# Second product of an attention kernel: low parts once for four units, not once for two

## The reference

```python
qkv = conv1d_same(group_norm(xf, gn_gamma, gn_beta), qkv_w, qkv_b)   # 3*256 x 256 x 16 taps
q, k, v = jnp.split(qkv, 3, axis=1)
w = jnp.einsum('bct,bcs->bts', q * scale, k * scale)                 # scores, 1024 x 1024 a head
w = jax.nn.softmax(w, axis=-1)
h = jnp.einsum('bts,bcs->bct', w, v)                                 # the second product
h = conv1d_same(h, proj_w, proj_b)
```

## Time and profile before

| | before |
|---|---|
| median of 3 runs | 1106.17 us (1106.09 to 1107.38) |
| profiled execution | 1104.99 us, of which span 1103.2 us |
| PE busy | 987.4 us, 90% |
| DVE busy | 716.3 us, 65% |
| ACT busy | 650.2 us, 59% |
| POOL busy | 233.4 us, 21% |
| mean granted TensorE clock | 0.965 |

### The profile page before, as it was taken

How to read it: one execution, slowest core, us unless ns; L and a number is a source line. 1 busy time by engine, 2 the same in 40 slices (tenths; PEclk the granted TensorE clock), 3 DMA queues, 4 the chain that set the end, 5 groups by cost and what they waited for, 6 DMA issues and landing times.

```text
span 1103.2 us, 18112 instructions
## 1 busy us (share of the span) xinstructions
PE 987.4 (90%) x7250; PEld 684.0 (62%) x7250; DVE 716.3 (65%) x1222; ACT 650.2 (59%) x1049; POOL 233.4 (21%) x164
## 2 busy tenths in 40 slices
PE   2888649999999999999598999999999999988864
PEld 1555526667766776667366666766677668766654
DVE  5988557654775577668466555465536665777767
ACT  4673617664676477767565565465636575665532
POOL 2736122100330132124050000010001004313320
PEclk9998879999999999999799999999999999999987
DMA  7050033593459357737644284537445873453522
GB/s 272 13 180 1 1 125 65 99 212 68 91 111 247 51 118 168 165 67 146 171 77 86 47 185 106 87 63 182 93 67 110 201 167 73 97 124 59 115 58 77
DMA packets 284515, 122.59 MB, mean 111 GB/s; under 512 B 268304, under 2 KB 270736, under 8 KB 283536
## 3 DMA queue, kind: packets, MB, share of 16 engines
q1 hardware_dynamic: 284432, 121.44, 49.5%
HBM read 34.24 MB, written 15.87 MB: 45 GB/s over the span
## 4 chain that ended last, share of the span: by engine, by line
PE 59%; DVE 11%; ACT 8%; issue 7%; DMA 2%; POOL 1%; SPq 0%; ACTq 0%; POOLq 0%; DVEq 0%
PE cM L1049 15%; PE cQ L1049 14%; PE cP L1049 13%; PE psT L1118 4%; PE psV L1095 4%; PE psS L1118 4%; PE psV L1099 3%; ACT arena L909 2%; DVE smx L1495 2%; DVE W L1280 1%; DMA arena<-arena 1%; DVE arena L1472 1%; PE cM L990 1%; ACT arena L921 1%; PE cP L990 1%
## 5 line engine op out<-in xcount | busy, mean ns | idle before, releaser
L1049 PE MATMUL cP<-U,W 128*128 128x256 f16 (+1 forms) x1536 | 224.3, 303 | 13.8 <-DVE W L1280 12.5
L1049 PE MATMUL cM<-U,W 128*128 128x256 f16 (+1 forms) x1536 | 223.3, 301 | 11.4 <-DVE U L1309 7.4
L1049 PE MATMUL cQ<-U,W 128*128 128x256 f16 (+1 forms) x1536 | 225.6, 302 | 5.7 <-DVE W L1280 3.5
L1049 PEld LDWEIGHTS cP<-U,W 128*128 128x128 f16 x1536 | 150.7, 98 | 82.0 <-issue 11.6
L1049 PEld LDWEIGHTS cM<-U,W 128*128 128x128 f16 x1536 | 149.6, 98 | 81.1 <-issue 8.9
L1049 PEld LDWEIGHTS cQ<-U,W 128*128 128x128 f16 x1536 | 149.7, 98 | 74.2 <-issue 6.0
L1472 DVE SCALAR_TENSOR_TENSOR arena<-arena,smx 128x1024 f16<-128x1024 f32 x128 | 178.5, 1394 | 1.3 <-ACT arena L921 0.6
L902 ACT ACTIVATE smx<-smx,esc 128x1 f32<-128x1 f32 x128 | 37.5, 293 | 207.4 <-DVE smx L1495 207.0
L921 ACT ACTIVATE arena<-arena,smx 128x1024 f16<-128x1024 f32 x128 | 147.0, 1148 | 4.2
L1495 DVE TENSOR_REDUCE smx<-psS 128x1 f32<-128x1024 f32 x64 | 77.9, 1217 | 71.5 <-PE psS L1118 71.1
L1495 DVE TENSOR_REDUCE smx<-psT 128x1 f32<-128x1024 f32 x64 | 78.0, 1219 | 57.1 <-PE psT L1118 56.7
(11 more groups left out here) (212 smaller groups left out, 1202.1 us busy)
## 6 DMA issues: line engine op xcount, KB each, us to landing
staging<-w_qkv SPq DMA_DIRECT2D x20, 512.0 KB, 5.1
kept_u<-U SPq DMA_DIRECT2D x4, 2077.0 KB, 10.0
U<-kept_u SPq DMA_DIRECT2D x16, 519.2 KB, 4.4
arena<-x_tok SPq DMA_DIRECT2D x8, 512.0 KB, 6.4
arena<-arena SPq DMA_DIRECT2D x16, 256.0 KB, 3.8
W<-x_tok SPq DMA_DIRECT2D x4, 1024.0 KB, 6.1
out_tok<-W SPq DMA_DIRECT2D x3, 1024.0 KB, 4.3
kept_h<-arena SPq DMA_DIRECT2D x4, 514.0 KB, 4.2
```

The costliest lines, as they stand in the source:

```text
L1049: last = mm(out, W[:, j, wl, c, wat + tap, :], U[:, slot, ul, c, at:at + width], start=(c == 0 and tap == 0 and wl + ul == 0), stop=(c == ...
```

## The change

An even h does its 8 full-width matmuls and returns. The odd h does its own 8, and then the 64-column ones of both halves, 16 in a row. No matmul is added or left out. The start flag is now set only with the first half, since a start marks all of the bank that the two halves share, and the first half's sum is still open when the second begins. `pv_done` is counted by 2 at the odd h in place of 1 at each. Nothing else is changed: the waits on `pv_done` keep their values.

```diff
                 for s in range(8):
-                    mm(psV[:, at:at + QUART], vT[:, s, hd, :], probT[:, s, at:at + QUART], start=(s == 0), stop=False,
+                    mm(psV[:, at:at + QUART], vT[:, s, hd, :], probT[:, s, at:at + QUART], start=(s == 0 and at == 0), stop=False,
                        skip_group_check=True)
-                for s in range(8):
-                    R = D * (s % 2)
-                    last = mm(psV[R:R + D, at:at + QUART], vT[:, s, hd, D * hd:D * (hd + 1)], probT[:, 8 + s, at:at + QUART],
-                              start=False, stop=(s >= 6), skip_group_check=True)
-                last.then_inc(S["pv_done"], 1)
+                if h % 2 == 0:
+                    return
+                for at in (0, QUART):
+                    for s in range(8):
+                        R = D * (s % 2)
+                        last = mm(psV[R:R + D, at:at + QUART], vT[:, s, hd, D * hd:D * (hd + 1)], probT[:, 8 + s, at:at + QUART],
+                                  start=False, stop=(at > 0 and s >= 6), skip_group_check=True)
+                last.then_inc(S["pv_done"], 2)
```

## The result

| | before | after |
|---|---|---|
| median | 1106.7 us (1106.09 to 1107.38, 4 runs) | 1125.74 us (1124.51 to 1126.43, 4 runs) |
| ratio | | 1.0177, 95% interval 1.0165 to 1.019 |
| span of the profiled execution | 1103.2 us | 1122.7 us |
| PE busy | 987.4 us | 985.6 us |
| mean granted clock | 0.965 | 0.960 |

The forecast was 1117.4 us, with a range up to 1122.5. The sign and the places of the main losses were right, the size was not: +19.5 us of span in place of +11.2.

A forecast was written before the change was run, and what follows sets the result against it. PE was taken to bound runs 0, 1, 2, 4, 5 and 6. Terms -5.0 + 7.2 + 7.8 + 1.2 = +11.2 us on the profiled 1104.99, plus 1.2 for the median, gave 1117.4 us; range 1109 to 1122.5.

The forecast's parts named there:

- The saving on PE: PE, 24 groups of four units in runs 0, 1, 2, 4, 5, 6: 0.21 us saved a group, 5.0 us in all.
- The turns wait for the odd h: SP: turns 4, 8 and 12 wait two slots longer, for h = 1, 3 and 5; turn 4 starts 8 us late.
- Unit 8's wait: PE, unit 8's scores: wait 1.2 us for the copy behind late turn 4, in six runs, 7.2 us.
- Run 2: Second half of load_w(4) behind late turn 12: squares and PE's spread 5.8 us later, plus 2 for clock, 7.8 us.
- Run 3: load_w(5) behind turn 5, which waits for its own low part; PE waits there anyway: 0 (to +1) us.
- Runs 0, 1 and 6: Late turns 8 and 12 were taken as covered, their next reader four slots on; no loss counted for this.
- Run 7: Last h = 7 at half clock with four more pairs, 0.9 us, plus 0.3 for a longer h = 5: 1.2 us.
- the 0.3 for h = 5: Run 7: h = 5 gets 0.44 us longer ahead of the last unit's scores; 0.3 of it counted.
- more comes late: Bunched transfers slow one another, turn 5 misses h = 2, or clock falls: 1 us more in six runs, 1123.4; chance 0.10.

The follow-up runs named there:

- the merged order alone: Changed kernel's matmul order, but even halves' 64-column matmuls read a stable tile, with pv_done counted by 1 at each h as before: 1101.77 us, ratio 0.9967.
- the kernels with the moves: Copy, run 3's and run 2's loads, stores and reload of runs 0 and 1, run 6's residual reordered: on the changed kernel 1097.05 us, on the kernel before 1098.87.
- the three kernels with a single move: Changed kernel with one reordering: copy ahead of turn 4, 1116.14 us; run 2's load ahead of turn 12, 1120.17; run 6's residual behind turn 14, 1122.74.
- The merged kernel with the moves: Changed kernel with copy, run 3's and run 2's loads, stores and reload of runs 0 and 1, run 6's residual reordered: 1097.05 us; 1096.68 on another chip.

## Why the prediction was too low

- **The saving on PE: right.** 0.21 us a group were forecast, 0.23 measured without the waits, 0.92 us a run where PE is the bound, 0.5 us more in six runs than I had counted. The Trainium skill ("TensorEngine Tiling (Array Packing)", Key Properties) says that a change of tiling mode drains the engine; with a full drain a group would have saved 0.32 us. The measured 0.23 is below it, as the rows had said; the 0.27 us of the last matmul, on which the 0.32 rests, is an end that the profile models.
- **The turns wait for the odd h: right**, to 0.1 us.
- **Unit 8's wait: right, a little low.** 1.2 us forecast, 1.09 to 1.26 printed in runs 0, 1, 2, 4, 5, 6. But I had worked out a delay of the scores' start, and that is 1.38 us: in run 5 they start 6.08 us behind the end of h = 1 in place of 4.70. The view counts idle time from the end of the last matmul, 0.16 us (0.27 - 0.109) after the next could have started. Taking the wait away gave 1.4 us a run in runs 4 and 5. Six times the 0.2 is 1.1 us of the missing sum.
- **Run 2: right.** 5.8 us on ACT forecast, 5.56 of wait there; the whole term 7.8 forecast, 8.15 measured by taking it away. The parts were both a little low: PE's wait grew by 6.5 and not 5.8 us (0.5 of it comes with the merged order alone), and PE then worked for 4.8 us at a granted clock of 0.50 (482.2 to 487.0), which is 2.4 us lost and not 2.
- **Run 3: wrong.** The step was "The one in run 3 follows turn 5, which waits for its own low part; PE waits there anyway, and I take 0 (to +1)". Both halves failed. Turn 5 does not start much later, but it stands close behind turn 4, the copy and an input quarter, and takes 3.94 us in place of the 1.84 that it had. And the wait on PE was the effect of that very load, not a cover: ACT waited 8.0 us for it before and 10.44 after. Measured: +2.5 us.
- **Runs 0, 1 and 6: wrong, of the same kind.** The step was "Turns 8 and 12 have their next reader four slots on, as turn 4 has". I followed the late turn and not the one behind it. Once turn 12 is late, turn 13 follows it and a 1 MB load without a pause, and h = 6 waits for 13, not 12: 2.18 us in run 6. The late turn 12 alone was not enough: with the 1 MB moved away h = 6 does not wait. In runs 0 and 1 turns 10 and 11 come behind turns 8 and 9 and a 2 MB store; h = 5 waits 0.74 and 0.26 us. That these are the queue and not PE is shown by the kernels with the moves, in which all three waits are gone (and another, before h = 7 of run 6, has come with the residual). The 0.74 of run 0 stands in one trace of a run that varies by 1.1 us, but it comes again as 0.70, 0.49 and 0.48 in the three kernels with a single move.
- **Run 7: near, and in part by luck.** 1.2 us forecast, 1.8 measured, but from other parts. The last block:

```profile
1073.14 1.86 PE L1095 MATMUL psV<-arena 128*128 128x256 f16 x8 [6.49 <-DMA arena<-arena]
1074.93 1.92 PE L1102 MATMUL psV<-arena 128*64 128x256 f16 x16
```

  1.92 us for the 16 against 1.06 for the 8 in the earlier trace rows, 0.86 of the 0.9 that I counted. Of the 0.3 for h = 5 only 0.1 came: the last h = 7 starts 129.29 us after the run's first scores before and 129.40 after, and within 0.2 of that in every kernel here. The rest goes with the clock. The 12 us from the start of the last h = 7, in the kernel before, the changed one, and the one with the late count alone (third number from the end is the clock):

```profile
1055.26:1067.26 12.00, 9.20 (x61) 6.66 (x62) 7.34 (x31) 3.29 (x6) 0.00 (x0) 0.64 0.01 1
1073.14:1085.14 12.00, 9.20 (x54) 6.30 (x55) 6.59 (x26) 3.29 (x6) 0.00 (x0) 0.53 0.01 1
1077.88:1089.88 12.00, 9.20 (x49) 6.14 (x50) 7.34 (x31) 3.29 (x6) 0.00 (x0) 0.52 0.00 1
```

  The third kernel has from there on the same matmuls as the kernel before, and takes 49.25 us to the end in place of 47.92: 1.3 us, at 0.52 in place of 0.64. The merged kernel with the moves took 48.78 and 49.86 us in its two profiles, at 0.60 and 0.51. So the merging costs some 0.9 us there, as forecast, and up to some 1.3 more go with the clock, which my sum for run 7 did not hold. What decides the clock in one execution or another stays open.
- **The rival "more comes late" is what happened.** I gave it 0.10 and 6 us; its mechanism (bunched turns, copy and input quarters slow one another) was the right one, at other places than I named: turn 5 did not miss h = 2 in any run. Nor was it 1 us in each of six runs: runs 4 and 5 had 0.1, run 3, which I had left out, 2.5.

The measured excess is 19.5 - 11.2 = 8.3 us: 2.5 in run 3, 2.4 in run 6, 1.6 in runs 0 and 1, 1.0 in run 2, 0.6 in run 7, 0.2 in runs 4 and 5.

## What to carry to other kernels

A semaphore that is counted less often releases later, and in a queue that is worked in order the price is paid by what stands behind the waiting entry; go through the queue entry by entry, with the time that each takes when it has no pause before it, until one starts at its old time again; and that one can still be slower for the transfer directly ahead of it, as turn 15 was. A long wait of the bounding engine is no cover before one knows what ends it: if the delayed transfer is at its root, each microsecond counts in full, and an earlier transfer is a gain to be had (here 5 us, more than the change was worth). And a small saving on the bounding engine can be kept, if the transfers that some engine needs soon are issued ahead of the entry that now waits.

## What I had not expected of the hardware

A DMA transpose of a unit takes 1.82 to 1.92 us in SP's queue in the rows above in which the queue was idle before it, but 3.94 and 4.12 us when it follows a transpose, a copy and a load without a pause. The earlier trace rows held the same already, 3.78 us close behind an input quarter, and I used the number without asking which other turns would come to stand like that. Over all 128 turns: in the kernel before, 9 start within 0.5 us of the end of the entry ahead, with a median of 3.78 us; in the changed one 54 do, with a median of 3.47; the others have a median of 1.85 in both. Whether the missing pause or the transfers still under way make the difference, no run here separates. The median over all 128 went from 1.86 to 1.94 us while the longest went from 8.1 to 10.7. The source view of the turns, after: duration in the queue (ns, least, median, most), and who waited for their landing:

```profile
L434 SPq DMA_TRANSPOSE arena<-arena x128: 1317/1942/10732, 174.8 to 1068.8; - x128
...
  ACT arena L921: 8.0, 11
  PE psV L1095: 7.5, 3
```

Where such an entry stands matters as much as how much it moves.
